# An adaLN block with a decayed-attention layer and a Sinkhorn-mixing layer: one batch at a time instead of both side by side

## The reference, cut to what matters

```python
x = hidden_states                                   # (2, 512, 512): two batches
sa, ca, ga, sb, cb, gb = modulation of layer 0      # silu(c) @ wmod, 6 rows of 512 per batch
h = layernorm(x) * (1 + ca) + sa
x = x + ga * L0_attn(h)                             # below
h = layernorm(x) * (1 + cb) + sb
x = x + gb * (h @ (wscale * sign(weight) + wbias).T)
sa, ca, ga, sb, cb, gb = modulation of layer 1
h = layernorm(x) * (1 + ca) + sa
x = x + ga * L1_attn(h)         # 32 heads of 16, 8 kv heads, rope, softmax(q k^T / 4) v
h = layernorm(x) * (1 + cb) + sb
x = x + gb * L1_ffn(h)          # 4 streams of 128, mixed by a 4x4 matrix per token:
                                # 50 Sinkhorn iterations on rmsnorm(h) @ W_res.T, and a branch

def L0_attn(h):                 # 32 heads of 128, 8 kv groups of 4 heads, 4 chunks of 128 tokens
    q, k = rope(h @ Wq.T), rope(h @ Wk.T); v = h @ Wv.T
    dt = softplus(h @ Win.T + dt_bias); G = cumsum(-dt * exp(A_log)) in each chunk
    y = (q k^T * exp(G_i - G_j), causal) (v dt) + (q exp(G)) state
    state = state * exp(G_last) + (k exp(G_last - G))^T (v dt)
    y = rmsnorm(y) * gnorm_w * silu(h @ Wg.T)
    return y @ Wo.T
```

## Time and profile before

| | us |
|---|---|
| median of 3 runs | 1672.2 |
| lowest and highest | 1672.09, 1673.42 |
| profiled execution | 1669.84 |
| its span, first to last instruction | 1667.9 |
| PE busy in the span | 1309.1 (78%) |
| PEld (weight load of PE) | 896.2 (54%) |
| DVE busy | 1128.4 (68%) |
| ACT busy | 674.6 (40%) |
| POOL busy | 784.7 (47%) |

### The profile page before, as it was taken

One profiled execution on the slowest core, in us unless ns is written; L12 is line 12 of the kernel. 1 busy time (PEld: TensorE's weight loads), 2 busy tenths in 40 slices (PEclk: granted clock), 3 DMA queues, 4 the chain that ended last, 5 costly groups with the idle time before them and its releaser, 6 DMA issues. The chain is left out here.

```text
span 1667.9 us, 19815 instructions
## 1 busy us (share of the span) xinstructions
PE 1309.1 (78%) x6320; PEld 896.2 (54%) x6320; DVE 1128.4 (68%) x2511; ACT 674.6 (40%) x1275; POOL 784.7 (47%) x721
## 2 busy tenths in 40 slices
PE   2768999999999999999999995675998579873000
PEld 0547767767767767777777674454222542223000
DVE  5644665556655666555566657795886859888998
ACT  0323433433334334334334331116476355774642
POOL 2237656765665757567566566561001600004244
PEclk8889999999999999999999998886799758995555
DMA  5211122122122121211221112300000000000001
GB/s 170 57 54 39 51 75 73 49 70 83 51 64 77 51 70 57 71 44 58 64 63 52 51 53 105 126 1 0 2 2 1 1 1 1 2 1 1 1 13 38
DMA packets 68215, 76.91 MB, mean 46 GB/s; under 512 B 5944, under 2 KB 40056, under 8 KB 68112
## 3 DMA queue, kind: packets, MB, share of 16 engines
q1 hardware_dynamic: 66240, 72.92, 14.3%
q10 hardware_dynamic: 1872, 2.72, 0.4%
HBM read 73.15 MB, written 2.28 MB: 45 GB/s over the span
## 5 line engine op out<-in xcount | busy, mean ns | idle before, releaser
L1085 DVE TENSOR_REDUCE nm<-bank 128x1 f32<-128x512 f32 x256 | 166.8, 677 | 17.1 <-PE bank L657 16.7
L1332 ACT ACTIVATE yTh<-yF 128x512 fp32r<-128x512 f32 x64 | 40.4, 632 | 330.6 <-DVE yF L940 330.6
L1520 POOL TENSOR_TENSOR sw<-sw,sinT 128x512 f32<-128x512 f32 x80 | 103.1, 1288 | 139.9 <-ACT sw L1283 139.9
L1532 POOL TENSOR_TENSOR dec<-gb,gcol 128x512 f32<-128x512 f32 x64 | 70.7, 1105 | 204.8 <-DVE Sd L906 190.7
L548 PE MATMUL bank<-st,qt 128*128 128x128 f32 x384 | 83.0, 301 | 61.6 <-DVE Sd L906 46.0
L878 DVE SCALAR_TENSOR_TENSOR gs<-tg,bank 128x512 f32<-128x512 f32 x64 | 44.0, 688 | 117.8 <-ACT tg L1290 117.8
L496 PE MATMUL bank<-hTh,wgh 128*128 128x512 f32 x256 | 121.3, 474 | 0.0
L657 PE MATMUL bank<-ksT,qsT 96*128 96x512 bf16 x256 | 112.5, 449 | 8.3 <-DVE nm L1085 3.1
L496 PE MATMUL bank<-hTh,wqh 128*128 128x512 f32 x256 | 107.1, 419 | 0.0
L576 PE MATMUL bank<-woh,yTh 128*128 128x512 f32 x256 | 104.4, 408 | 2.7 <-DVE yTl L943 2.7
L548 PEld LDWEIGHTS bank<-st,qt 128*128 128x128 f32 x384 | 66.7, 211 | 71.1 <-DVE Sd L906 50.1
(11 more groups left out here) (298 smaller groups left out, 3701.8 us busy)
## 6 DMA issues: line engine op xcount, KB each, us to landing
gb<-g_scr SPq DMA_DIRECT2D x64, 256.0 KB, 3.5
raw<-in_wmod SPq DMA_DIRECT2D x40, 256.0 KB, 2.7
raw<-in_wo SPq DMA_DIRECT2D x32, 256.0 KB, 2.8
raw<-in_wq SPq DMA_DIRECT2D x31, 256.0 KB, 2.7
raw<-in_wg SPq DMA_DIRECT2D x31, 256.0 KB, 2.7
mt<-mods_scr SPq DMA_DIRECT2D x20, 256.0 KB, 6.9
stg<-in_wmod SPq DMA_DIRECT2D x2, 1024.0 KB
xin<-in_x SPq DMA_DIRECT2D x8, 256.0 KB, 7.2
```

What stands on the lines that cost most here:

```text
L1085: ve.tensor_reduce(nm[:, i, h:h + 1], banks[bk][:, :], AX.X, ALU.max, negate=True).then_inc(*v_nm.up(b, h, i))
L1520: po.tensor_tensor(s_[:, :], s_[:, :], sinT[:, :], ALU.mult).then_inc(*g_rope.up("sin", kind, t, n))
L1532: po.tensor_tensor(dec[:, :, :], gb[s % 2][:, :, :], bc(gcol[:, t % 2, heads(t), n], 2, 128), ALU.subtract).then_inc(*g_dec.up("sub", s))
```

## The change

The order of the loop is turned around: turns 0 to 7 (slots 0 to 31) are the eight kv groups of batch 0, turns 8 to 15 those of batch 1.

- Weights are split in turns 0 to 7 alone, 14 tiles in four slots where it was 14 in eight. q, g, k and v tiles go through a ring of four hi/lo pairs (`ring`), `wo` has four pairs of its own. `keep_ring` and `keep_o` write each hi and lo tile (256 KB each) to a DRAM tensor `w_scr` of 112 tiles; for batch 1, `fetch_ring` and `fetch_o` read them back (two loads of 256 KB a tile), with no split. All these are issued by SyncE.
- `qT`, `gs`, `ktok` and `vtok` have one buffer for two. The projections rotate over two banks for three; scores and state update share bank 2, and the transposes (of y, k and v) share bank 4 with the `wo` sum. The g pieces run three slots ahead. Both turns of k and v (`turn_kv`) stand in the slot n = 3, right before `fold_b`.
- The twelve modulation blocks (`mod_quad`, `mod_rows`) and the FFN's weights are spread over slots 1 to 28 (`beside_first`).
- All of batch 0's second half (`beside_second`: front, attention, head, Sinkhorn of four tiles with the branch, finish) is spread over slots 33 to 63, by estimated costs (`Pace`: after each third matmul group of a piece or fold, as many steps as are due). It uses PSUM banks 5 and 6 in rotation, for both kinds of score tiles and everything else, and 7 for pv.
- After the loop the second half of batch 1 runs by itself.

Its core, as a diff:

```diff
-NG = KVH * B
+NTURN = KVH * B
...
-    pbank = (0, 1, 2)
-    bS, bY, bC, bT, bO = 3, 4, 5, 6, 7
+    pbank = (0, 1)
+    bS, bY, bT = 2, 3, 4
+    use_of = ({"w": (6, 7), "turn": (5, 6), "ffn": (5, 6), "q": (5, 6), "k": (5, 6), "part": (5, 6), "A": (5, 6), "B": (5, 6), "pv": (7,),
+               "T": (5, 6), "br": (5, 6)},
+              {"turn": (1, 2), "ffn": (0, 5), "q": (3, 5), "k": (4, 2), "part": (6, 7), "A": (0, 1, 7), "B": (3, 4, 5), "pv": (6,),
+               "T": (2,), "br": (0, 1)})
...
+        def tick(self):
+            while self.spent * self.places < self.n * self.all:
...
+        def keep_ring(self, k, n):
+            sp, (hi, lo), at = self.e, ring[k % NRING], kept(*proj[k])
+            sp.wait_ge(*v_wl(n))
+            sp.dma_start(d_w[at, 0], flat(hi).bitcast(F32)).then_inc(*d_keep[k % NRING].up(k, "hi"))
+            sp.dma_start(d_w[at, 1], flat(lo).bitcast(F32)).then_inc(*d_keep[k % NRING].up(k))
...
+        def fetch_ring(self, k):
+            sp, (hi, lo), at = self.e, ring[k % NRING], kept(*proj[k])
+            sp.wait_ge(*p_proj(*proj[k - NRING]))
...
+            sp.dma_start(flat(hi).bitcast(F32), d_w[at, 0]).then_inc(*d_ring[k % NRING].up(k, "hi"))
+            sp.dma_start(flat(lo).bitcast(F32), d_w[at, 1]).then_inc(*d_ring[k % NRING].up(k))
...
+    def beside_second(E):
+
+        yield from front(E, 0, 8)
+        yield from attention(E, 0)
+        yield from head(E, 0)
+        yield from mixes(E, 0)
+        sk, br = stream(E, sinkhorn, 0, 0, 4), stream(E, branch, 0)
+        both = merged(sk, br)
...
+        yield from finish(E, 0)
...
     def layer0_loop(E):
         E.load_gb(0), E.load_gb(1)
         E.prep(0), E.prep_exp(0), E.prep2(0)
-        for _ in range(4):
-            E.split()
+        E.prepare_o(0)
         for s in range(NSLOT):
...
+            if s == 1:
+                E.pace = Pace(stream(E, beside_first), sum(places(x) for x in range(1, 28)))
...
+            if s == 33:
+                E.pace = Pace(stream(E, beside_second), sum(places(x) for x in range(33, NSLOT)))
             E.scores(s)
-            if ahead:
+            if s + 1 < NSLOT:
                 E.prep(s + 1)
+            if t + 1 < NTURN:
+                E.piece("q", t + 1, n)
             if s:
                 E.fold_a(s - 1)
-            if more:
-                E.piece("q", t + 1, n)
             E.outputs(s)
...
-            if more:
-                E.piece("g", t + 1, n)
+            if s + 3 < NSLOT:
+                E.piece("g", (s + 3) // 4, (s + 3) % 4)
             E.state(s)
...
-            if more and n == 0:
-                E.piece("k", t + 1, 0)
-            if more and n == 1:
-                E.piece("v", t + 1, 0)
-                E.turn_k(t + 1)
-            if more and n == 2:
-                E.turn_v(t + 1)
+            if t + 1 < NTURN and n in (1, 2):
+                E.piece("kv"[n - 1], t + 1, 0)
+            if t + 1 < NTURN and n == 3:
+                E.turn_kv("k", t + 1)
+                E.turn_kv("v", t + 1)
...
             if s:
                 E.fold_b(s - 1)
-            if s in mod_at:
-                E.mod_block()
-            for _ in range((4 if s % 8 == 0 and s > 0 else 0) + (todo_at.get(s % 8, 0) if s // 8 + 1 < KVH else 0)):
-                E.split()
-            if s >= NSLOT - 5:
-                second_half(E, s)
+            if n == 0 and s:
+                E.prepare_o(t)
...
     def story(E):
         layer0_head(E)
-        layer0_loop(E)
...
+        rest = layer0_loop(E)
+        merged(stream(E, front, 1, 6), rest).rest()
+        stream(E, attention, 1).rest()
+        stream(E, head, 1).rest()
         E.mix_y(1)
         sk1 = merged(stream(E, sinkhorn, 1, 0, 2), stream(E, sinkhorn, 1, 2, 4))
-        merged(taken(sk1, 28), pending).rest()
-        merged(taken(sk1, 212), stream(E, branch, 1)).rest()
-        merged(sk1, stream(E, finish, 0)).rest()
+        taken(sk1, 28).rest()
+        merged(sk1, stream(E, branch, 1)).rest()
         stream(E, finish, 1).rest()
         E.end()
```

More of the change, by code:

```diff
@@ L48, with __init__, step, rest @@
     reciprocal = bn_stats = bn_aggr = affine_select = same
+class Stream:
+    def __init__(self, steps, costs):
+        self.steps, self.costs, self.at = steps, costs, 0
+        self.left = len(costs)
+    def step(self):
+        if self.left == 0:
+            return 0
+        self.left -= 1
+        self.at += 1
+        next(self.steps)
+        return self.costs[self.at - 1]
+    def rest(self):
+        while self.step():
+            pass
+def taken(a, n):
+    def steps():
+        while a.step():
+            yield 1
+    return Stream(steps(), a.costs[a.at:a.at + n])
+def merged(a, b):
+    na, nb = a.left, b.left
+    order, k = [], 0
+    for i in range(na):
+        order.append((a, a.costs[a.at + i]))
+        while k * na < (i + 1) * nb and k < nb:
+            order.append((b, b.costs[b.at + k]))
+            k += 1
+    order += [(b, c) for c in b.costs[b.at + k:]]
+    def steps():
+        for x, _ in order:
+            x.step()
+            yield 1
+    return Stream(steps(), [c for _, c in order])
+def joined(*parts):
+    def steps():
+        for p in parts:
+            while p.step():
+                yield 1
+    return Stream(steps(), [c for p in parts for c in p.costs[p.at:]])
+class Pace:
+    def __init__(self, stream, places):
+        self.stream, self.places, self.n = stream, places, 0
+        self.all, self.spent = sum(stream.costs), 0
+    def tick(self):
+        self.n += 1
+        while self.spent * self.places < self.n * self.all:
+            c = self.stream.step()
+            if not c:
+                return
+            self.spent += c
 def bc(ap, axis, n):
@@ new lines, in scores, with outputs, fold_a, fold_b @@
+        def scores(self, s):
+            self.scored(s)
+            self.drain[bS] = v_Sd(s)
+        def outputs(self, s):
+            self.output(s)
+            self.tick()
+            if s % 4 < 3:
+                self.states(s)
+                self.drain[bS] = v_st(s)
+            self.tick()
+            self.drain[bY] = v_norm("yn", s)
+        def fold_a(self, s):
+            self.folded_a(s)
+            self.drain[bT] = v_yF(s)
+        def fold_b(self, s):
+            for h in range(4):
+                self.folded_b(s, h)
+                self.tick()
+            self.drain[bT] = v_acc(s)
@@ new lines, in attention, with run @@
+    def attention(E, b):
+        def run(s):
+            while True:
+                c = s.step()
+                if not c:
+                    return
+                yield c
+        yield from parts(E, b, 4)
+        yield from turns(E, b, 4)
+        yield from parts(E, b, 0)
+        yield from turns(E, b, 0)
+        yield from run(merged(stream(E, line_a, b, 0), stream(E, parts, b, 1)))
+        yield from turns(E, b, 1)
+        for u in range(4):
+            if u < 2:
+                yield from run(merged(stream(E, line_b, b, u), joined(stream(E, line_a, b, u + 1), stream(E, parts, b, u + 2))))
+                yield from turns(E, b, u + 2)
+            elif u == 2:
+                yield from run(merged(stream(E, line_b, b, u), stream(E, line_a, b, 3)))
+            else:
+                yield from line_b(E, b, 3)
@@ new lines, in norms, with head @@
+    def norms(E, of, b):
+        i0 = 4 * b
+        for i in (i0, i0 + 1):
+            E.moments(of, i), (yield 1)
+        for i in range(i0, i0 + 4):
+            if i + 2 < i0 + 4:
+                E.moments(of, i + 2), (yield 1)
+            E.rows(of, i), (yield 1.4)
+    def head(E, b):
+        i0 = 4 * b
+        ns = norms(E, "h", b)
+        E.residual("h", i0), (yield 1)
+        E.residual("h", i0 + 1), (yield 1)
+        yield next(ns)
+        E.residual("h", i0 + 2), (yield 1)
+        yield next(ns)
+        E.residual("h", i0 + 3), (yield 1)
+        yield from ns
+        for j in range(6):
+            if j < 4:
+                E.square(i0 + j), (yield .5)
+            if j >= 2:
+                E.logits(i0 + j - 2), (yield .6)
+            if 1 <= j < 5:
+                E.turn_l(i0 + j - 1), (yield .6)
+                E.rms(i0 + j - 1), (yield .3)
@@ L2119, in starts @@
[L2119 to L2126 removed]
+        return rest
     def story(E):
         layer0_head(E)
[L2130 to L2144 removed]
+        rest = layer0_loop(E)
```

2025 lines of the change are left out of this document (1018 added, 1007 removed), and 3 rows, old and new, of the table q_at.

## The result

The changed kernel takes 1788.2 us (median of 4 runs), the one before 1672.7: a ratio of 1.070, interval 1.067 to 1.073. Slower, as forecast, but by 115 us where 66 were forecast: inside the prediction's outer bounds of 1625 to 1805, and 8 us above the 1700 to 1780 that its forecast gives. The profiled execution has a span of 1785.5 us. Its stages, in the columns of the earlier trace rows (stretch, length, busy PE, PEld, DVE, ACT, POOL, PEclk, DMA share, GB/s): head, slots 0 to 32, slots 33 to 54, slots 55 to the last fold, the tail.

A forecast was written before the change was run, and what follows sets the result against it. TensorE bounds the loop's 61 slots; VectorE's program-order queue already costs it time. Head 103.7 + slots 545 + 497 + 208 + last fold 8 + tail 372 = 1733.7, plus 1.9 and 2.4: 1738 us, range 1700 to 1780.

The forecast's parts named there:

- Head, 103.7: The stretch up to the start of the first scores, claimed unchanged at 103.7 us.
- Slots 0 to 32, 545: Loop slots with all splits, modulations and weight turns: 483.5 us of TensorE work plus waits, 545 us, bounds 505 and 580.
- The bursts of `wo` splits: In n==0 slots of slots 0 to 32, VectorE's splits outlast TensorE's work: eight at 4.6 us idle, 37 us.
- The chain of k and v in bank 4: In n==3 slots, turns, copies and fold_b use bank 4 one after the other: 1.6 us times eight, 13 us.
- Slots 33 to 54, 497: Loop slots beside batch 0's front, attention and head: 442 us of TensorE work plus waits, 497 us, bounds 455 and 560.
- Two banks: Batch 0's work in slots 33 to 54 has two rotating banks, drains queue: 3.5 us per slot in 16 attention slots.
- Slots 55 to the fold, 216: Loop end with batch 0's Sinkhorn in VectorE's queue: slots 55 to 63 at 208 us, last fold 8.
- `T` ops: Sinkhorn multiplications in slots 55 to 63, slowed beside POOL: 95 at 0.2 us more, 20 us; 36 by the skill's rule.
- Tail, 372: Batch 1's second half alone after the loop: 372 us, bounds 350 and 395, where both batches together took 604.
- Loads: Rival: transfers make the ring late in half of slots 0 to 32, 50 us more, 1790 us; chance 0.10.
- Overlap nearly free: Rival: slots 33 to 54 keep 0.7 us idle a slot, Sinkhorn fits in 165; 1605 us plus 4; chance 0.20.
- Sinkhorn outside the loop: Rival: part of batch 0's Sinkhorn falls after slot 63, front of batch 1 grows; 1725 to 1750 us; chance 0.05.

The follow-up runs named there:

- experiment 1: Against the changed kernel, batch 0's second half leaves slots 33 to 63 and runs by itself after the loop, ahead of batch 1's; median 1972.2 us.
- experiments 5, 7 and 8: Against the change: batch 0's maxima over 64 columns, 1773.3 us; one bank per kind, 1829.2. Against experiment 1: a stop in slots 36 to 55, 376.0 for 281.8.
- experiment 2: Against the changed kernel, tiles of kv groups 1 to 7 store 32 of 512 columns and batch 1 fetches group 0's tiles; median 1790.7 us.
- experiment 4: Against the changed kernel, batch 0's Sinkhorn, branch and finish leave the loop and stand beside batch 1's attention; median 1772.1 us.

## Why the prediction was right or wrong

- **The account of the whole.** By experiment 1 the loss of 117.6 us in span is: 4.0 in the head, 9.2 in the loop's own time (543.8 + 425.7, for 960.3 before), and 104.4 in the second halves: 328.8 beside the loop and 379.5 after it, where before both together took 603.9. Before, the halves of the two batches filled each other's gaps, on all banks: two such halves one after the other would be about 757 us (an estimate, twice the 378.6 of batch 1's in experiment 1), and the pair took 603.9. The change splits this pair; batch 1's half is left with nothing beside it (TensorE busy 193 of 379.5 us), and batch 0's stands beside an engine with almost no gaps. There it costs 50 us less than such a half by itself on six banks, and losing the pair costs 153. That the tail would give back 232 us and the loop take more was the prediction's frame, and it held (224 and 338).
- **Head, 103.7**: 107.7. Its runs here spread from 107.7 to 112.6, and the first scores wait 3.87 us for POOL's rotation; not pursued.
- **Slots 0 to 32, 545**: 543.8, right in sum and wrong in its parts. The bursts of `wo` splits, priced at 37 us, cost about 11 (an estimate, from four of the eight): they run at the start of the slots with n = 1, and the slots 17, 21, 25 and 29 took 16.2, 16.3, 16.5 and 16.1 us, with some modulations and weight turns among them, for the 14.9 of a slot with n = 1 and without splits in experiment 1. That is at most 1.6 a burst and not 4.6. Slot 13 took 22.8 with 6.2 us idle; what did it there was not looked into. The chain of k and v in bank 4 took 16.6 for 13. Slots 0 and 1 took 47.8 us with 31 of TensorE's work: the start cost 17 by itself, and not a part of 12. The rest is in single waits of up to 7.9 us. No wait for the ring is among them.
- **Slots 33 to 54, 497**: 561.8, the step that failed, as a size. "TensorE work 442" was 485.8 busy, and "55 idle" was 76. (16 slots at 3.5 us are 56, which leaves nothing for the front's six, though the text says that 497 is with the front's.) Idle time: 21 us more than priced. The prediction had `nm` and the exp in its price (20.8 us in 19 waits), and nothing for the copies of q and k (17.6 in 3) or the front's `hh` on POOL (7.5 in 3). Busy time: a price for the clock was missing. The granted clock is at the lower level in twelve stretches, 71.7 us in all, and TensorE is busy for 55.7 of them, which costs 28 of the 44 us. Another 3 are the loop's own matmuls (busy 299.9 us in these slots of experiment 1, at a clock of 1.00, for 297 priced) and 2 the first fp32r matmul behind a pv, 20 times 0.34 for 0.23 us; the other 11 stay open. That it is the stops is what experiments 5, 7 and 8 show: fewer or shorter, and both idle and busy time fall; a bank less, and both rise.
- **Two banks**: named as a cause, priced too low. One bank a kind costs 41 us more; six banks make an attention by itself a matter of 149 us from first to last score tile, for 247 on two. The prediction had the wait for a bank in its price, and not the clock behind it.
- **Slots 55 to the fold, 216**: 192.7. VectorE did carry the chain: it was busy 117.5 of the 141.7 us of slots 55 to 61, 83% where 85 or more was the sign. These seven slots came out 36 us under the 178 priced, and slots 62, 63 and the fold took 51 for 38. The waits for `Sd` of 8 us and more that were to show there are 1.3 us in all; TensorE waited most for the bank that the turns share with the `wo` sum (`acc`, 18.0 us in 6 waits to the end of the fold). The 87 `T` ops from 1213 to 1343 us:

```profile
L1367 DVE TENSOR_TENSOR T<-P,a 128x64 f32<-128x64 f32 x45 | 15.1, 336 | 1.4
L1367 DVE TENSOR_TENSOR T<-P,b 128x64 f32<-128x64 f32 x42 | 13.7, 325 | 1.3
```

  At 0.22 each they would be 19.1 us; the excess is 9.7 for the 20 taken. By the rule of the Trainium skill, "SBUF — State Buffer", section "Who interferes with whom", the prediction made it 36 as an estimate. The rule shows in the trace, and the product was too high: POOL is busy 42% of this stretch, not 64, and only 24 of the 87 `T` ops were lengthened, by 0.40 us on the mean. Each of these 24 began while a POOL op was running and ended 0.08 us after that op's end, as here (1240.71 and 1240.79):

```profile
1239.66 1.05 POOL L1725 TENSOR_TENSOR dec<-gb,gcol 128x512 f32<-128x512 f32 x1 [6.09 <-DVE Sd L1125]
1240.27 0.52 DVE L1367 TENSOR_TENSOR T<-P,b 128x64 f32<-128x64 f32 x1
```

  Fifteen others overlap a POOL op and took 0.22 us, nine of them beside the small `rsm` of 4 columns.
- **Tail, 372**: 379.5. Front to the first transposes of q and k 75.7 for 67; from there to the last pv 163 as said; head 32 for 34; the rest 108.3 as said.
- **The rivals.** Loads (0.10): out by experiment 2. Overlap nearly free (0.20): out, slots 0 to 63 and the fold took 1298 us and not 1141. Sinkhorn outside the loop: didn't happen; tried on purpose (experiment 4) it gains 16 us, about as much as the 13 at the edge of what was given for it.

## What to carry to other kernels

A full engine has almost no gaps to fill: work put beside it costs its own engine time in full (the front's 176 matmuls 34 of its 40 us), and the stops that it brings can cost TensorE half as much again in clock. It can still be cheaper than the same work by itself (the front 40 us for 83, attention and head 188 for 217), so what has to be compared is the place that it has now: two halves that wait on different engines and stand beside each other were worth 153 us here (the estimate above), and no version won that back. Before moving a stage, ask what fills its gaps now, and how many banks it will rotate over at the new place.
